# Delta rule: where the value projections of a unit are computed

## What is computed

```python
Q = (x @ Wq).reshape(B, T, H, D)
K = (x @ Wk).reshape(B, T, H, D)
V = (x @ Wv).reshape(B, T, H, D)
beta = jax.nn.sigmoid(x @ Wbeta + b_beta)
K = K / jnp.maximum(jnp.linalg.norm(K, axis=-1, keepdims=True), EPS)

def step(W, inp):
    q_t, k_t, v_t, b_t = inp
    pred = jnp.einsum('bhij,bhj->bhi', W, k_t)
    err = v_t - pred
    W_new = W + b_t[..., None, None] * jnp.einsum('bhi,bhj->bhij', err, k_t)
    o_t = jnp.einsum('bhij,bhj->bhi', W_new, q_t)
    return (W_new, o_t)
```

## Time and profile before

| | us |
|---|---|
| median of 3 runs | 1617.49 |
| lowest, highest | 1614.69, 1625.23 |
| the profiled execution | 1627.39 |
| its span in the profile | 1625.6 |
| PE busy, mean granted clock | 1469.5 (90%), 0.973 |
| PEld, DVE, ACT, POOL busy | 802.6, 1122.3, 925.9, 695.2 |
| chain that ended last: PE, DVE, ACT, issue, POOL | 61%, 17%, 10%, 6%, 4% |

### The profile page before, as it was taken

How to read it: one execution, slowest core, us unless ns; L and a number is a source line. 1 busy time by engine, 2 the same in 40 slices (tenths; PEclk the granted TensorE clock), 3 DMA queues, 4 the chain that set the end, 5 groups by cost and what they waited for, 6 DMA issues and landing times.

```text
span 1625.6 us, 44178 instructions
## 1 busy us (share of the span) xinstructions
PE 1469.5 (90%) x19224; PEld 802.6 (49%) x19224; DVE 1122.3 (69%) x2297; ACT 925.9 (57%) x1301; POOL 695.2 (43%) x736
## 2 busy tenths in 40 slices
PE   8888888899999999999987989799999989999996
PEld 4222222333335333433433545678777778775553
DVE  6677776888875785767555677666776765574664
ACT  2687776678876875777584333364556544342220
POOL 2111130566655665666483104468756667001010
PEclk9898999999999999999999999899999999989998
DMA  4000002333322232233120100000000001100000
GB/s 163 1 1 1 1 0 89 93 96 101 89 76 76 78 91 76 76 105 92 34 73 16 68 1 14 15 16 4 17 17 17 17 4 39 54 2 1 5 9 14
DMA packets 32417, 70.79 MB, mean 44 GB/s; under 512 B 5328, under 2 KB 7056, under 8 KB 31968
## 3 DMA queue, kind: packets, MB, share of 16 engines
q1 hardware_dynamic: 32224, 67.98, 14.3%
HBM read 47.45 MB, written 20.51 MB: 42 GB/s over the span
## 4 chain that ended last, share of the span: by engine, by line
PE 61%; DVE 17%; ACT 10%; issue 6%; POOL 4%; DMA 0%; ACTq 0%; DVEq 0%; POOLq 0%
PE ps L160 59%; DVE a_MX L432 4%; ACT b_X L957 3%; POOL b_EL L975 2%; ACT b_EH L169 2%; DVE b_mx L895 1%; PE ps L242 1%; POOL d_XI L1779 1%; POOL d_tmp L1776 1%; ACT b_Hk L169 1%; DVE b_rd L1067 1%; DVE b_VL L830 1%; DVE c_SG L1398 1%; DVE b_Lk L836 1%; DVE c_H L1404 1%
## 5 line engine op out<-in xcount | busy, mean ns | idle before, releaser
L975 POOL TENSOR_TENSOR b_EL<-b_X,b_EH 128x1024 f16<-128x1024 f32 x160 | 341.0, 2131 | 215.0 <-ACT b_EH L169 214.8
L957 ACT ACTIVATE b_X<-ps 128x1024 f32<-128x1024 f32 x160 | 163.7, 1023 | 108.2 <-PE ps L160 106.9
L1776 POOL TENSOR_TENSOR d_tmp<-d_G,d_XI 128x31 f32<-128x31 f32 (+15 forms) x248 | 126.6, 511 | 162.4 <-DVE d_G L1705 143.5
L432 DVE TENSOR_REDUCE a_MX<-ps 128x2 f16<-128x1024 f32 x128 | 155.3, 1227 | 57.2 <-PE ps L160 56.5
L895 DVE TENSOR_REDUCE b_mx<-ps 128x2 f32<-128x1024 f32 x128 | 156.0, 1219 | 55.7 <-PE ps L160 53.9
L169 ACT ACTIVATE b_EH<-b_X 128x1024 f16<-128x1024 f32 x160 | 169.1, 1057 | 25.5 <-PE ps L160 14.3
L160 PE MATMUL ps<-b_M,b_S 128*64 128x512 f16 (+1 forms) x1408 | 177.0, 383 | 3.1 <-ACT b_X L957 3.0
L469 ACT ACTIVATE a_E<-ps 128x1024 f32<-128x1024 f32 x128 | 131.1, 1024 | 58.3 <-PE ps L160 57.8
L1779 POOL TENSOR_TENSOR d_XI<-d_XI,d_tmp 128x31 f32<-128x31 f32 (+15 forms) x248 | 139.6, 563 | 19.4
L160 PEld LDWEIGHTS ps<-b_M,b_S 128*64 128x64 f16 (+1 forms) x1408 | 69.1, 108 | 86.5 <-issue 21.6
L451 POOL TENSOR_TENSOR a_QS<-a_QS,a_MR 128x512 f16<-128x512 f16 x16 | 18.5, 1156 | 213.8 <-ACT a_MR L169 209.6
(11 more groups left out here) (321 smaller groups left out, 3304.6 us busy)
## 6 DMA issues: line engine op xcount, KB each, us to landing
b_S<-s_xk SPq DMA_DIRECT2D x48, 336.0 KB, 6.4
b_M<-s_xq SPq DMA_DIRECT2D x48, 256.0 KB, 5.0
s_xk<-b_Hk SPq DMA_DIRECT2D x16, 336.0 KB, 2.2
s_xk<-b_Lk SPq DMA_DIRECT2D x16, 336.0 KB, 2.5
s_xq<-b_Hq SPq DMA_DIRECT2D x16, 256.0 KB, 2.0
s_xq<-b_Lq SPq DMA_DIRECT2D x16, 256.0 KB, 2.0
d_XI<-eye SPq DMA_DIRECT2D x8, 512.0 KB, 3.5
f_w<-f_w SPq DMA_DIRECT2D x1, 2048.0 KB, 8.4
```

What stands on the lines that cost most here:

```text
L432: v.e.tensor_reduce(out, PS[:, bk:bk + 2, :], AX, ALU.max).then_inc(sem("a_mx"), 1)
L957: a.e.activation(b_X[k % 2], PS[:, bk:bk + 2, :], ACT.Exp, scale=0.125).then_inc(sem("b_ex"), 1)
L975: last = p.e.tensor_tensor(b_EL[k % 6], b_X[k % 2], b_EH[k % 6], ALU.subtract)
L1776: e.tensor_tensor(tm, a, x, ALU.mult).then_inc(*p.step())
```

## The change

`values` gets the unit as an argument, on PE and on DVE. Unit 0's two groups stay where they were. Those of unit u+1 are issued within unit u's preparation: group 0 behind the solves and ahead of the transitions, group 1 between the transitions and the steps. The steps stand one `yield` later than before, the number of `yield`s is the same. On DVE the same groups stand ahead of and behind the four `d_AT` instructions. ACT's order and the other queues are unchanged.

```diff
@@ d_prep_tensor
-            def values(k):
+            def values(u, k):
+                x, w = d_XS[u // 4 % 2], 256 * (u % 4)
                 bk = ringD.take(t, ("dv", u, k), 1, "d_v", 2 * u + k + 1)
...
-            values(0)
+            if u == 0:
+                values(0, 0)
             yield
             queries(0)
             yield
-            values(1)
+            if u == 0:
+                values(0, 1)
             yield
...
             for k in range(4):
                 solve(k)
                 yield
+            if u + 1 < 16:
+                values(u + 1, 0)
             yield
             update("da", "d_a", "d_am", 64, 128, 1, 6, transitions)
             yield
+            if u + 1 < 16:
+                values(u + 1, 1)
+            yield
             update("db", "d_b", "d_bm", 64, 128, 0, 6, steps)
-            yield
             yield
@@ d_prep_vector
-            def values(k):
+            def values(u, k):
+                m, j = u // 2, u % 2
+                KV = d_KV[m % 3]
                 s = d_sb[:, m % 4].rearrange("p (c h) -> p c h", c=4)[:, 2 * k:2 * k + 2, 4 * j:4 * j + 4]
+                v.wait_ge("d_kn", 4 * m + 4)
                 v.wait_ge("d_vm", 2 * u + k + 1)
...
-            values(0)
-            yield
-            yield
-            values(1)
+            if u == 0:
+                values(0, 0)
+            yield
+            yield
+            if u == 0:
+                values(0, 1)
             yield
...
+            if u + 1 < 16:
+                values(u + 1, 0)
             v.wait_ge("d_am", u + 1)
...
                 last.then_inc(sem("d_a"), 1)
+            if u + 1 < 16:
+                values(u + 1, 1)
             yield
```

## The result

| | before | changed |
|---|---|---|
| median of 21 runs each | 1622.66 us | 1628.72 us |
| lowest and highest | 1614.69, 1631.63 | 1622.89, 1636.53 |
| profiled execution, its span | 1627.39, 1625.6 us | 1628.72, 1626.9 us |

The ratio is 1.0035, 95% interval 1.002 to 1.005: 5.7 us slower, inside the range and in the class "same", but three times the +1.9 us that the sum gave. The profiled execution of before was 4.7 us above its median, that of the changed kernel is its median, so the two spans hide most of the difference; it is read stage by stage.

A forecast was written before the change was run, and what follows sets the result against it. PE was taken to bound the delta rule, busy 380.4 of 415 us. Terms -2.5, +4.0, -0.3 and +0.7 sum to +1.9 us on a base of 1617.5, rounded to 1619.5 us; range 1607 to 1631.

The forecast's parts named there:

- the class "same": Whole kernel: a difference under 1% (16 us) either way, between 1601.3 and 1633.7 us; chance 0.86.
- What bounds the kernel, and what the stalls are: Delta rule: PE busy 380.4 of 415 us; 18.7 us of issue stalls are late 256-instruction blocks in small-matmul bursts.
- a block is usable some 3.0 to 3.9 us after the one before it is entered: PE instruction fetch: block requested when the previous one is entered; full-speed bursts, 2.05 us per 256 instructions, therefore starve.
- Plain passes: Unit 0's preparation and u = 1, 3, 5, 7, 9, 11 to 14: 0.25 us won each, ten times, -2.5 us.
- The 0.35 that I priced as lost: Plain passes: reads start 0.35 us late because DVE does 0.76 us of values ahead of its d_AT.
- Turn passes: u = 2, 4, 6, 8, key rows behind: +4.0 us in all; u = 0 and 10 are the other turn passes.
- with both stalls (2.4 us) swallowed by these waits: Turn passes on PE: new DVE waits absorb both issue stalls, so d_wo starts only 0.9 us later.
- I take +1.0 us each, 4 × 1.0: Turn passes u = 2, 4, 6, 8: ACT's later d_XE copies delay d_NW, +4.0 us in all; bounds 0 and 2.2 each.
- rival 2: ACT's queue becomes the path: d_XE lateness passes on whole, 8 to 14 us slower; sign: d_NW,d_X gap 2 us or more; chance 0.17.
- The two small terms: Turn passes u = 10, -0.3 us by PE's own path, and u = 0, +0.7 us, from 0 to 1.4.
- Rival 1: The bursts are relieved: issue stalls and d_UW, d_KT waits shrink, 8 to 13 us faster; chance 0.20.
- Rivals 3 and 4: 3: waits traded one for one, 1617.5 us, chance 0.08. 4: stalls are not fetches, 12 us lost, 1631.5 us, chance 0.05.

The follow-up runs named there:

- hold6: The kernel before plus six useless 128x256 matmuls per unit between reads and outputs; ratio 0.9981, median 1619.7 us.
- its control: The kernel before plus six useless 128x256 matmuls per unit, ahead of the first query projection; ratio 1.0033, median 1627.0 us.
- dve_order: The changed kernel with, on DVE only, group 0 a step earlier and group 1 a step later; ratio to the kernel before 0.9947, median 1615.3 us.
- split_groups: The changed kernel with group 0 a step earlier on DVE, group 1 between reads and outputs (DVE: behind the d_QT subtraction); ratio to the kernel before 0.9947.

## Why the prediction was right in class and too small in size

**What bounds the kernel, and what the stalls are: right.** `hold6`, its control and the packets show it. That a block is usable some 3.0 to 3.9 us after the one before it is entered was too strong: the changed kernel's stall ends at 1163.07, 256 instructions after 1159.91; the same 256 in `dve_order` run from 1157.27 to 1159.45, 2.2 us, without a stall. The figure fits where the packet begins late (3.2 us here), as counted from the matmuls. Issue, forecast at about 8 us in all, stayed at 12.8. The Trainium skill, "Runtime: NRT & Kernel Launch", section "Instruction fetch mechanics", says that the next page is fetched while the current one runs, and that the crossing is mostly hidden. The traces agree that the packet moves while the block before runs; on the hiding they don't: 18.7 us of the stage before, 12.8 after.

**Plain passes: the signs right, -2.5 us forecast, about 0 measured.** The `d_UW` wait went, the transitions follow without a gap, and a stall of 0.75 us stayed where 0.6 to 1 was written (0.49 to 0.97 over passes 1 to 11). In passes 1, 3, 5 and 9 the sum is -0.20 to -0.37, as forecast (-0.25). It was multiplied by ten; unit 0, pass 7 and above all pass 11 (+0.92) gained nothing or lost. The 0.35 that I priced as lost, because the reads would go late behind `d_AT`, was not lost there: `d_AT` was done at 1160.37, the first read began at 1160.61 without idle time, and no wait for `d_AT` stands in the stage. That pass 3 came out at -0.24 all the same is luck: by the tables its idle time fell by 0.55 us (20.29 less 18.95, against 20.05 less 19.26), and PE's busy time grew by 0.31, for which the sum has no term. The steps' wait for group 0's bank was named and got no price; it shows no idle time, and where it costs, it does so in the stall behind.

**Turn passes: the named waits right, the price mis-sized twice.** Forecast were about 1.4 us for `d_KV` (measured 1.22 to 1.56), 1 for `d_L` (0.28 to 0.74) and 1 or more for `d_NW` (0.60 to 1.18), 0.2 for `d_KT` (0.23). First failure: "with both stalls (2.4 us) swallowed by these waits". 0.45 and 0.55 us of them stayed in pass 6, so that `d_wo` began 1.8 us later in its pass (1241.68 less 1220.50, against 1241.20 less 1221.80) and not 0.9. That did not reach the sum, which goes by ACT's path: there the `d_XE` copies were forecast 2.2 us late and came 2.32 late (1243.44 less 1220.50, against 1242.42 less 1221.80). Second failure: "I take +1.0 us each, 4 × 1.0", worked out on pass 6, whose ACT had idle pieces. For pass 6 it is exact (+1.09), though not by the reading given: the 5.17 us of the table count overlaps once, so ACT was idle for 0.59 us there and not 0.9. In pass 4 ACT had none, which the trace of before showed. ACT from its `d_XE` copies to `d_NW` in passes 4 and 6 of the kernel before (busy us, instructions, clock, DMA share, GB/s):

```profile
1193.66:1200.25 6.59, 6.55 (x12) 1.00 0.25 80
1242.42:1250.51 8.09, 7.29 (x14) 1.00 0.22 68
```

0.04 us of idle in the one, 0.80 in the other. The same stretch of pass 6 took 6.88 us in the changed kernel, 1.21 less, with ACT busy for 6.82: 0.74 came out of idle time and 0.47 from instructions that lay closer together, which the forecast had no term for. In the changed kernel's pass 4, ACT's timeline:

```profile
1192.86 2.12 ACT L169 ACTIVATE d_XE<-d_XE 32x1024 f32<-32x1024 f32 x2
...
1199.32 1.19 ACT L1927 ACTIVATE d_NW<-ps 32x512 f32<-32x512 f32 x2
```

From the start of the piece (1169.63, before 1172.86) the copies are 2.43 us later and `d_NW` 2.30, and the piece is 2.30 longer. That is rival 2, in which the lateness passes on whole: it held at passes 4 and 8, the case taken as likeliest at 6, and pass 2 lies between (+1.40). Four passes at 1.0 should have been two near 1.2 and two near 2.3, a little over the bound of 2.2. The two small terms were off as well: pass 0 took +1.77 where 0 to 1.4 was allowed, pass 10 -1.08 where -0.3 was written.

**Rivals.** Rival 1 failed for this change (issue 12.8, but new waits in its place) and is nevertheless within reach: it gave 8 to 13 us off, and `dve_order` and `split_groups` are both 8.6 us (0.53%) under the kernel before, 6.6 and 6.8 at equal clock. Rival 2 was half right, though the sign given for it, a gap of 2 us or more ahead of `d_NW,d_X`, never showed (1.18 at most); the two rows above would have told it from the main case. Rivals 3 and 4 fell.

**The conclusion on the change.** The move itself is good and its place in DVE's queue is not. One step earlier there for group 0 and one later for group 1 turn +0.35% into -0.53%; the version that wins most is that or `split_groups`, which can't be told apart.

## What to carry to other kernels

When work is moved on one engine, move its partner on the engine that frees its buffer with the same care: with the same order on PE this kernel was 0.35% slower or 0.53% faster than before, by DVE's order alone. A per-pass price worked out on one pass has to be looked up in each kind of pass before it is multiplied, above all the idle time of the engine that is to absorb the lateness. And a wait with no idle time in the trace may still cost, where the next block of instructions comes late for it; three of six passes here fit that.

## What the runs showed of the hardware

- A block of 256 PE instructions ran in 2.2 us without a stall when its successor's packet began 0.1 us behind the first step, and stalled for 0.75 us when it began 1.2 us behind it, with the same instructions on PE. Over the twelve plain passes looked at in the two kernels, packets 0.04 to 0.12 us behind went with stalls of 0 to 0.20 us, packets 0.59 to 1.17 us behind with 0.48 to 0.97.
- 10 us of added matmuls inside starving bursts made the kernel no slower (0.9981, and +0.7 us at equal clock), the same matmuls elsewhere cost 5.4 us.
- PE's clock fell to 1.2 GHz behind idle times, but not behind each long one. In the changed kernel `d_NW,d_X` (64 matmuls) took 1.20 us in pass 6 and, behind 1.51 us of waiting for `d_X`, 1.68 at the start of pass 1's piece, where the granted clock is 0.92:

```profile
1096.75 1.68 PE L160 MATMUL ps<-d_NW,d_X 32*32 32x32 f32 x64 [1.51 <-DVE d_X L1988]
```

  A wait of 1.18 us was followed by a fall at 1305 and by none at 1200, so that the pieces behind them, passes 9 and 5, took 21.67 us (granted clock 0.92) and 19.85 (1.00). In the kernel before, stalls of 1.59 us at 1240 and 1.81 at 1290 were followed by none. What is read from one profiled pass has to be freed of such a fall (1.7 us) first.
- Over 269 executions of fourteen kernels, 0.001 less in the mean granted clock went with 1.1 us more of 1620.
